# Layer 1's FFN in two passes with batched roots, and the node rows loaded during the sort

## The reference

```python
# first graph layer: z = layernorm(x) @ W0, then
x = x + segment_sum(z[src] * edge_weight[:, None], dst, 2500)
# first FFN (ternary weights: w = unit * {-1, 0, 1})
h = layer_norm(_layernorm(x)) * ln1_g + ln1_b
h = gelu(h @ w1.T + b1)                  # 1024 -> 512, exact gelu
h = layer_norm(h) * ln2_g + ln2_b
x = x + h @ w2.T + b2                    # 512 -> 1024
# second graph layer: scores per node from the normalised x and att = W1 * (a_l, a_r)
xn = _layernorm(x);  el, er = scores(xn);  ...
```

## Time and profile before

| | us |
|---|---|
| median of 3 runs | 3577.93 (3573.08 to 3578.49) |
| the profiled execution | 3581.93 |
| its span, first to last instruction | 3580.2 |

### The profile page before, as it was taken

One profiled execution on the slowest core, in us unless ns is written; L12 is line 12 of the kernel. 1 busy time (PEld: TensorE's weight loads), 2 busy tenths in 40 slices (PEclk: granted clock), 3 DMA queues, 4 the chain that ended last, 5 costly groups with the idle time before them and its releaser, 6 DMA issues. The chain is left out here.

```text
span 3580.2 us, 50457 instructions
## 1 busy us (share of the span) xinstructions
PE 2847.5 (80%) x13602; PEld 2228.0 (62%) x13602; DVE 2455.1 (69%) x5351; ACT 1536.9 (43%) x3068; POOL 1714.2 (48%) x1564
## 2 busy tenths in 40 slices
PE   0996102999996777889899899999999699289996
PEld 0885101444443665877777588888887688278886
DVE  6222602999997665527777799999999564467774
ACT  1221000333333765523333377777776332055554
POOL 4777873666664221247777344444443111023332
PEclk9998555999998898579999899999999688599999
DMA  3333306999997011101111188887877332289997
GB/s 103 79 96 109 92 2 246 353 349 351 348 347 225 30 41 55 40 20 20 26 20 26 38 263 259 262 261 260 260 261 230 114 139 106 103 239 284 282 284 181
DMA packets 223841, 609.09 MB, mean 170 GB/s; under 512 B 47387, under 2 KB 85650, under 8 KB 223582
## 3 DMA queue, kind: packets, MB, share of 16 engines
q0 software_dynamic: 139008, 429.63, 38.7%
q1 hardware_dynamic: 84702, 177.85, 14.5%
HBM read 521.91 MB, written 85.11 MB: 170 GB/s over the span
## 5 line engine op out<-in xcount | busy, mean ns | idle before, releaser
L640 POOL DMA_INDIRECT g_rows<-z_rows,edge_src x704 | 700.4, 995 | 615.6 <-PE g_totals L1397 307.8
L705 PE MATMUL g_sums<-g_rows,g_share 128*128 128x512 f32 x704 | 333.0, 595 | 211.3 <-DVE g_goes L746 211.3
L483 POOL DMA_INDIRECT edge_list<-payload,row_i x320 | 402.3, 1257 | 144.1 <-issue 141.3
L691 ACT ACTIVATE g_scaled_hi<-g_rows,edge_weight_sorted 128x1024 fp32r<-128x1024 f32 x176 | 202.6, 1151 | 540.6 <-DMA g_rows<-z_rows,edge_src 505.4
L1051 POOL DMA_INDIRECT shared<-el_rows,edge_src x352 | 334.8, 951 | 178.8 <-issue 107.0
L1390 PE MATMUL g_sums<-g_rows,g_share 128*128 128x256 f32 x1408 | 348.9, 391 | 0.0
L705 PEld LDWEIGHTS g_sums<-g_rows,g_share 128*128 128x128 f32 x704 | 133.5, 190 | 312.3 <-DVE g_goes L746 211.7
L1342 ACT ACTIVATE g_scaled_hi<-g_rows,g_factor 128x256 fp32r<-128x256 f32 x704 | 299.9, 496 | 4.3 <-DMA g_rows<-z_rows,edge_src 3.2
L1466 DVE SCALAR_TENSOR_TENSOR g_scaled_lo<-g_rows,g_factor,g_scaled_hi 128x256 fp32r<-128x256 f32 x704 | 293.4, 479 | 1.1 <-ACT g_scaled_hi L1342 0.9
L1390 PEld LDWEIGHTS g_sums<-g_rows,g_share 128*128 128x128 f32 x1408 | 255.6, 191 | 27.6
L1245 DVE TENSOR_REDUCE t_largest<-t_masked 128x4 f32<-128x512 f32 x352 | 231.9, 685 | 55.7 <-PE t_masked L1117 49.4
(11 more groups left out here) (359 smaller groups left out, 7696.5 us busy)
## 6 DMA issues: line engine op xcount, KB each, us to landing
e_raw<-in_L_ffn_rw_dram SPq DMA_DIRECT2D x56, 1024.0 KB, 7.5
g_rows<-z_rows,edge_src POOLq DMA_INDIRECT x704, 5.7
z_rows<-z_zout SPq DMA_DIRECT2D x20, 512.0 KB, 2.9
x_rows<-x_all SPq DMA_DIRECT2D x20, 512.0 KB, 2.7
z_rows<-t_zout SPq DMA_DIRECT2D x20, 512.0 KB, 2.8
s_x<-x_rows SPq DMA_DIRECT2D x10, 1024.0 KB, 8.9
xn_rows<-s_rows SPq DMA_DIRECT2D x10, 1024.0 KB, 4.1
z_x<-in_x_dram SPq DMA_DIRECT2D x19, 512.0 KB
```

Source lines behind the costliest of these rows:

```text
L483: pool.indirect_dma_start(out=g.lists[k], out_offset=bass.IndirectOffsetOnAxis(ap=row_i[0:EP, c:c + 1], axis=0), in_=payload[0:EP, c, :], ...
L640: pool.indirect_dma_start(out=r.rows[:, slot, :], out_offset=None, in_=table, in_offset=bass.IndirectOffsetOnAxis(ap=g.src[:, i * GT + q:i ...
L705: nc.tensor.matmul(sums[:, k, h, :], share[:, k, :], r.rows[:, k * GT, h * HALF:(h + 1) * HALF], start=True, stop=False)
```

## The change

Four edits.

1. `x_all` is allocated before the sort stage. The projection's weights and its transposed tile are laid into the same memory. In the sort stage SyncE loads 19 of the 20 tiles after its last weight chunk, when the projection has ended; GpSimd clears the padding after its last scatter, SyncE then loads the last tile, and then the merged lists. The first graph stage has no loads and no wait on them.
2. The FFN makes two passes over the tiles, written out step by step with no loop. Pass 1 ends with Gelu and the statistics of `hidden`, which is kept for all tiles; pass 2 does the rest. Square roots are taken for several tiles at once: at steps 0, 2, 6, 12 for x, at steps 16 and 26 for hidden. The gains are multiplied on GpSimd ahead of the transposes; the shifts go through the weights once and into b1 and b2 (32 products at the start). ACT copies each transposed tile to hi in one instruction.
3. Pass 2 also takes the statistics of the finished x.
4. The score pass uses them: one root for all tiles, no statistics in the loop, and transposes alternate between `turned` and `z`, one tile ahead.

```diff
 PRODUCTS = 6 * KD
 Z_FIRST = 160
+FIRST_NORM = ((0, 3, 0), (3, 7, 2), (7, 13, 6), (13, 20, 12))
+FIRST_STATS = {0: (3, 4), 1: (5, 6), 2: (7, 8), 3: (9, 10), 4: (11,), 5: (12,), 6: (13, 14), 7: (15,), 8: (16,),
...
+        tile_bytes = 4 * D
+        w_hi = nc.alloc_sbuf_tensor_at("w0_hi", [P, KD, D], F32R, offset=g.x_at)
+        w_lo = nc.alloc_sbuf_tensor_at("w0_lo", [P, KD, D], F32R, offset=g.x_at + KD * tile_bytes)
+        z0_hi = nc.alloc_sbuf_tensor_at("z0_hi", [P, 2, KD, P], F32R, offset=g.x_at + 2 * KD * tile_bytes)
+        z0_lo = nc.alloc_sbuf_tensor_at("z0_lo", [P, 2, KD, P], F32R, offset=g.x_at + (2 * KD + 2) * tile_bytes)
+        r = projection_tiles(a, "z0", True, z0_hi, z0_lo)
...
+            sp.wait_ge(r.z_ready, NT)
+            sp.wait_ge(r.lo_ready, NT)
+            sp.dma_start(g.x_all[:, 0:NT - 1, :], g.x[0:(NT - 1) * P, :].rearrange("(t p) d -> p t d", p=P)).then_inc(x_in, 16)
+            sp.wait_ge(pads_ready, 1)
+            sp.dma_start(g.x_all[0:LAST, NT - 1, :], g.x[(NT - 1) * P:N_NODES, :]).then_inc(x_in, 16)
             for k in range(LISTS):
                 sp.wait_ge(scattered[k], 16 * (EC // LISTS))
                 if k == 3:
                     sp.wait_ge(merge_used, 1)
                 sp.dma_start(merged[:, (0, 1, 2, 1)[k]], g.lists[k].rearrange("(p t) k -> p t k", p=P)).then_inc(merged_in[k], 16)
+            sp.wait_ge(x_in, 32)
...
         @block.tensor
         def _(pe):
...
-        pads_ready, x_in = a.sem("g0_pads_ready"), [a.sem("g0_x_in0"), a.sem("g0_x_in1")]
         share_ready, added, scaled_ready, split_ready = (
             a.sem(f"g0_{n}") for n in ("share_ready", "added", "scaled_ready", "split_ready"))
         x_flat = g.x_all[:].rearrange("p t d -> p (t d)")
 
         block = ctx.enter_context(nc.Block())
 
-        @block.sync
-        def _(sp):
-            full = (NT - 1) * P
-            sp.dma_start(g.x_all[:, 0:NT - 1, :], g.x[0:full, :].rearrange("(t p) d -> p t d", p=P)).then_inc(x_in[0], 16)
-            sp.wait_ge(pads_ready, 1)
-            sp.dma_start(g.x_all[0:LAST, NT - 1, :], g.x[full:N_NODES, :]).then_inc(x_in[1], 16)
-
         @block.gpsimd
...
             v = nc.vector
-            dve.wait_ge(x_in[0], 16)
-            dve.wait_ge(x_in[1], 16)
...
-        def x_tile(it):
-            return x_flat[:, bass.ds(it.i * D, D)]
+        hidden = sb("hidden", [P, NT, HID])
+        rows2, hi2, lo2 = rows[:, :, 0:HID], hi[:, :, 0:KH, :], lo[:, :, 0:KH, :]
+        turned, h1 = a.psum("f0_turned", [P, 2, HALF]), a.psum("f0_h1", [P, 2, HID])
+        h2 = a.psum("f0_h2", [P, 2, 2, HALF])
...
+            sp.wait_ge(t1_ready, 1)
+            sp.dma_start(b2, g.b2.partition_broadcast(P)).then_inc(late_in, 16)
+            sp.dma_start(gain2, g.ln2_g.partition_broadcast(P)).then_inc(late_in, 16)
+            for n in range(NT):
+                sp.wait_ge(x_ready, n + 1)
+                sp.dma_start(g.x2[n * P:(n + 1) * P, :], g.x_all[:, n, :]).then_inc(stored, 16)
...
+            q = nc.gpsimd
+            q.tensor_copy(t2[:].rearrange("p c n -> p (c n)"), g.t2[:].rearrange("p c n -> p (c n)")).then_inc(t2_ready, 1)
+            pool.wait_ge(small_in, 64)
+            for s in range(STEPS):
+                n = tile_of(s, 1)
+                if n is not None:
+                    pool.wait_ge(rows_ready, n + 1)
+                    q.tensor_tensor(rows[:, n % 2, :], rows[:, n % 2, :], gain1[:], ALU.mult).then_inc(rows_scaled, 1)
+                n = tile_of(s, 1, 1)
+                if n is not None:
+                    if n == 0:
+                        pool.wait_ge(late_in, 32)
+                        pool.wait_ge(bias_ready, 2)
+                    pool.wait_ge(rows2_ready, n + 1)
+                    q.tensor_tensor(rows2[:, n % 2, :], rows2[:, n % 2, :], gain2, ALU.mult).then_inc(rows2_scaled, 1)
+                    q.tensor_tensor(g.x_all[:, n, :], g.x_all[:, n, :], b2, ALU.add).then_inc(shifted, 1)
...
+                if n is not None:
+                    k = n % 2
+                    pe.wait_ge(hi_ready, n + 1)
+                    pe.wait_ge(lo_ready, n + 1)
+                    if n == 0:
+                        pe.wait_ge(bias_ready, 1)
+                    at_least(pe, pre_ready, n - 1)
                     for c in range(KD):
-                        for n, part in enumerate((hi, lo)):
-                            mm = t.matmul(h1[:, k, :], part[:, k, c, :], t1[:, c, :],
-                                          start=c == 0 and n == 0, stop=c == KD - 1 and n == 1)
+                        for m, part in enumerate((hi, lo)):
+                            mm = t.matmul(h1[:, k, :], part[:, k, c, :], t1[:, c, :], start=c == 0 and m == 0,
+                                          stop=c == KD - 1 and m == 1)
                     mm.then_inc(h1_ready, 1)
...
+            for s in range(STEPS):
+                for k, (first, end, at) in enumerate(FIRST_NORM):
+                    if at == s:
+                        act.wait_ge(mv_ready, end)
+                        s_.activation(std[:, first:end], mv[:, first:end, 1], ACT.Sqrt, bias=eps_eps[:, 0:1],
+                                      scale=1.0 + EPS).then_inc(std_ready, 1)
+                for k, (first, end, at) in enumerate(SECOND_NORM):
+                    if at == s:
+                        act.wait_ge(mv2_ready, end)
+                        s_.activation(std2[:, first:end], mv2[:, first:end, 1], ACT.Sqrt,
+                                      bias=g.eps[:, 0:1]).then_inc(std2_ready, 1)
+                n = tile_of(s, 0)
+                if n is not None:
+                    act.wait_ge(rstd_ready, 1 + max(k for k in range(len(FIRST_NORM)) if FIRST_NORM[k][0] <= n))
+                    at_least(act, turned_ready, n - 1)
+                    s_.activation(rows[:, n % 2, :], g.x_all[:, n, :], ACT.Identity, bias=nmr[:, n:n + 1],
+                                  scale=rstd[:, n:n + 1]).then_inc(rows_ready, 1)
+                n = tile_of(s, 2)
+                if n is not None:
+                    act.wait_ge(turned_ready, n + 1)
+                    at_least(act, h1_ready, n - 1)
+                    s_.copy(hi[:, n % 2].rearrange("p k n -> p (k n)"),
+                            turned[:].rearrange("p h n -> p (h n)")).then_inc(hi_ready, 1)
+                n = tile_of(s, 4)
+                if n is not None:
+                    act.wait_ge(pre_ready, n + 1)
+                    s_.activation(hidden[:, n, :], hidden[:, n, :], ACT.Gelu).then_inc(hidden_ready, 1)
+                n = tile_of(s, 0, 1)
+                if n is not None:
+                    act.wait_ge(rstd2_ready, 1 if n < SECOND_NORM[0][1] else 2)
+                    if n < 2:
+                        act.wait_ge(turned_ready, NT)
+                    at_least(act, turned2_ready, n - 1)
+                    s_.activation(rows2[:, n % 2, :], hidden[:, n, :], ACT.Identity, bias=nmr2[:, n:n + 1],
+                                  scale=rstd2[:, n:n + 1]).then_inc(rows2_ready, 1)
+                n = tile_of(s, 2, 1)
+                if n is not None:
+                    act.wait_ge(turned2_ready, n + 1)
+                    if n < 2:
+                        act.wait_ge(h1_ready, NT - 1 + n)
+                    at_least(act, h2_ready, n - 1)
+                    s_.copy(hi2[:, n % 2].rearrange("p k n -> p (k n)"), turned[:, n % 2, :]).then_inc(hi2_ready, 1)
...
+            def first_stats(n):
+                at_least(dve, mv_ready, n - 1)
+                st.done(v.bn_stats(stats[:, n % 2, 0, :], g.x_all[:, n, 0:HALF]))
+                st.link(v.bn_stats(stats[:, n % 2, 1, :], g.x_all[:, n, HALF:D]))
+                v.bn_aggr(mv[:, n, :], stats[:, n % 2]).then_inc(mv_ready, 1)
+
...
+            for s in range(STEPS):
+                for k, (first, end, at) in enumerate(FIRST_NORM):
+                    if at == s:
+                        dve.wait_ge(std_ready, k + 1)
+                        scales(first, end, mv, std, rstd, nmr, rstd_ready)
+                for k, (first, end, at) in enumerate(SECOND_NORM):
+                    if at == s:
+                        dve.wait_ge(std2_ready, k + 1)
+                        scales(first, end, mv2, std2, rstd2, nmr2, rstd2_ready)
+                if s == 0:
+                    dve.wait_ge(bias_summed, 1)
+                    v.scalar_tensor_tensor(out=b1[:], in0=h1[:, 0, :], scalar=g.unit[:, 0:1], in1=b1[:], op0=ALU.mult,
+                                           op1=ALU.add).then_inc(bias_ready, 1)
+                if s == 1:
+                    dve.wait_ge(bias_summed, 2)
+                    dve.wait_ge(late_in, 32)
+                    v.scalar_tensor_tensor(out=b2, in0=h2[:, 0].rearrange("p h n -> p (h n)"), scalar=g.unit[:, 1:2],
+                                           in1=b2, op0=ALU.mult, op1=ALU.add).then_inc(bias_ready, 1)
+                n = tile_of(s, 2)
+                if n is not None:
```

(54 more changed lines are left out.)

314 lines of the change are left out of this document (107 added, 207 removed).

## The result

| | us |
|---|---|
| before, median of 4 runs | 3578.21 (3573.08 to 3578.56) |
| after, median of 4 runs | 3466.22 (3463.02 to 3471.35) |
| ratio | 0.9692, 95% interval 0.9675 to 0.9708 |
| span of the profiled execution, before and after | 3580.2 and 3462.7 |

The kernel is 112.0 us faster; 3471 was predicted. The profiled spans differ by 117.5 us, and the sum of the prediction, made between such spans, was 106.5. A second set of runs of the changed kernel (c0_after, 5 runs) gave 3468.42 us, 0.9690 (0.9673 to 0.9707), and its profiled span was 3469.5 us, 110.7 less than before.

A forecast was written before the change was run, and what follows sets the result against it. It saw a chain of stages between barriers, each with another limit. Terms −28, −56 and −22.5 make −106.5, from 3581.93 profiled to 3475.4; less 4.0 for the median, 3471 us, range 3445 to 3500 (chance 0.70).

The forecast's parts named there:

- Part 2: Layer 1's FFN in two passes with batched roots: 227 us against 283.5, −56 us.
- Part 1: Sort and first graph: node rows loaded during the sort remove the 39.7 us hole; −28 us (−13 to −31).
- The load beside the scatters: End of the sort: the node-row load slows GpSimd's scatters; cost taken as 3 us, between 0 and 18.
- The merged lists: End of the sort: their loads wait for GpSimd's fill, so the first addition comes 2.8 us later.
- pass 1 with its bubbles: FFN, first pass: 4.8 us a tile, 96 us for 20, plus 18 us of bubbles, mostly at batched roots.
- pass 2 with filling and last addition: FFN, second pass: 20 tiles at 4.4 us make 88, filling 2.5, last addition 1.7 us.
- GpSimd's price: FFN: a GpSimd operation takes 2.87 us on 1024 columns, half on 512, giving 4.4 us a tile in pass 2.
- Part 3: Score pass: statistics and roots out of the loop, a second bank so TensorE never waits; 103 against 125.8, −22.5 us.
- Rival 1: FFN: strictly ordered engine queues clash, steps of 6.3 and 5.2 us; +46, 3517 us; chance 0.13.
- Rival 2: Score pass: the clock rises, loads and products halve to 2.75 us; −40, 3431 us; chance 0.09.
- Rival 3: Sort and graph: load beside scatters costs its upper end, or gather ring starts ill-filled; +18, 3489 us; chance 0.05.
- Rival 4: FFN: TensorE stays at 1.2 GHz, 357 us against 283.5; kernel 3601 us; chance 0.03.

The follow-up runs named there:

- e1: Changed kernel with the node rows loaded and their padding cleared in the first graph stage again; 3925.14 us, 0.978 of before, on a chip that delays attention.
- e5: Changed kernel with the last tile's padding cleared by VectorE right behind the projection, not by GpSimd behind the last scatter; 3463.78 us, 0.9674 of before.
- e8: Changed kernel with added VectorE multiplications in eight FFN steps, four with two SBUF inputs, four with one PSUM input; 3905.75 us on a chip that delays attention.
- e2: Changed kernel with the old attention stage: statistics and roots tile by tile, one bank for transposes; 3926.56 us, 0.9794 of before, on a chip that delays attention.
- e10: Changed kernel with all score-pass tiles turned in one bank, statistics and roots still ahead; 3905.46 us, 0.973 of before, on a chip that delays attention.
- e3: Changed kernel with a square root for each FFN tile (first three together) instead of batches; 3940.21 us, 0.9817 of before, on a chip that delays attention.
- e6: Changed kernel with the attention vectors copied into PSUM, so VectorE's products in the sort read one SBUF input, not two; 3452.11 us, 0.9645 of before.

## Why the prediction came out as it did

Direction, size and the places were right. The sum of −106.5 was short by 11 us of the 117.5 between the two spans, and by 4 of the 110.7 with c0_after. Part 2 alone was short by 10 us in both.

- **Part 1, −28, measured −26.7 (−23.1 in c0_after).** Two errors, one against the other. The load beside the scatters was put at 3 us. Behind VectorE's last product, up to 453 us, the steps of the scatters are together 1.3 to 1.9 us above 1.49 us each in the eight traces with the load and unchanged scatters, and not at all in the two without it (before and e1). (The rule of the Trainium skill's page "DMA: Bandwidth & Descriptors", Arbitration, that a long transfer delays a short one by turns only, is borne out: under 2 of a possible 18 us.) The merged lists were put at 2.8 us later and came 8.7, 1.2 of it the last scatter's own: I spaced the loads as before, where each left as its scatters landed. Now three leave between 553.3 and 554.1, right behind the load of the last tile, and land at 561.7, 563.3 and 565.0, after 8.4 to 10.9 us and not 4.1 to 5.2 as before. The first addition needs two of them. e5 showed that this alone moves the first gather by 6.6 us. Together they put the first gather at 573.75 us (575.3 in c0_after) and not at 570.3. From the first gather's issue to the end of the graph it took 542.7 us (544.7 in c0_after), where 544.9 was put.
- **Part 2, −56, measured −66.3.** By its terms: start 17, measured 15.9; pass 1 with its bubbles (its pauses at the batches) 114, measured 110.4; pass 2 with filling and last addition 92, measured 87.2; the store 3.7 as put. The term that was most mis-sized is GpSimd's price, 2.87 us for 1024 columns. It made GpSimd the pace of pass 2, 4.4 us a tile; with the measured 2.41 and 1.30 GpSimd needs 3.7, and TensorE's 4.18 is the pace, near the low bound of 4.1. That is 4.3 us of the 9.7 over 20 tiles. The others are 1.8 us by the step of pass 1 (4.71 for 4.8), 1.8 by its bubbles, 1.1 at the start and 0.7 at the ends of pass 2. The price was taken from a row in whose stage VectorE runs an operation with two SBUF inputs on every tile (lo out of cols and hi); the change itself removes that operation, since lo is now taken from PSUM. e8 showed the mechanism, and the trace of before shows its size:

```profile
1156.45 2.35 POOL L814 TENSOR_TENSOR x_all<-x_all,f_b 128x1024 f32<-128x1024 f32 x1 [8.41 <-ACT f_rows L895]
...
1177.90 1.22 DVE L957 TENSOR_TENSOR f_lo<-f_cols,f_hi 128x1024 fp32r<-128x1024 f32 x1
...
1178.45 2.91 POOL L814 TENSOR_TENSOR x_all<-x_all,f_b 128x1024 f32<-128x1024 f32 x1 [6.25 <-ACT f_rows L895]
```

  GpSimd's first addition met no such operation and took 2.35 us. The other 19 overlapped it by 0.57 to 0.68 us and took 2.83 to 2.94. There as in e8 the operation is longer by the overlap less some 0.17 us, so the overlap accounts for the whole step from 2.41 to 2.87.
- **Part 3, −22.5, measured −22.8.** e2 confirms the size. That the number fits so well is partly luck: in this trace the clock was high for the first score products, which gave 1.6 us; in c0_after it was not, and the part is −21.2. The reason was half wrong: e10 gives 1.6 us to the second bank, which I had named as what frees TensorE.
- **Rivals.** Rival 1 (orders that clash): the steps are TensorE's, and what is left of it is the bubbles, 13 us in pass 1. e3 shows that it is real where roots are taken one by one: the queue's order costs 12.5 us in a pass whose tables change only at its head. Rival 2 (the clock rises in the scores): it did not stay up. In nine of the twelve traces of the new pass the clock is 0.50 throughout, with PE busy 101.7 of 102.4 us in c0_after. In three (after, e1 and e6) it was high for a moment at the head, with products 0.11 us apart, and fell while TensorE went on without a pause; the first trace of the changed kernel (columns as in the table of stages; the granted clock is the third number from the end):

```profile
1337.10:1341.40 4.30, 3.31 (x16) 3.07 (x16) 1.60 (x4) 3.38 (x4) 0.00 (x0) 0.67 0.58 203
1341.40:1343.00 1.60, 1.46 (x14) 1.49 (x14) 0.79 (x1) 1.60 (x2) 0.00 (x0) 1.00 0.04 10
1343.00:1437.90 94.90, 94.90 (x456) 94.90 (x456) 29.04 (x59) 44.33 (x43) 18.84 (x8) 0.50 0.11 34
```

  Rival 3 (the load beside the scatters): 1.3 to 1.9 us of 18. Rival 4 (the low clock in the FFN): the FFN had 0.94.

## What to carry over

A duration taken from a trace holds beside the work of that trace: before it is used in a sum, ask whether the change removes what ran next to it. When a wait is put into a queue, price what stands behind it by how it will leave, all at once, and not by the spacing it had. And a reason that yields the right number is not yet shown: the bank and the batches each needed a run of its own.
